# Third layer's attention: queries in the weighted heads' bank, probabilities scaled on GpSimd, keys first at the beginning

## The reference

```python
x = x + jnp.tanh(g_xattn[2]) * _L2_xattn_ref(_layernorm(x, axis=-1), ctx_2048, Wq, Wk, Wv, Wo)

def _L2_xattn_ref(inputs_q, inputs_kv, Wq, Wk, Wv, Wo):
    H, HD = (16, 128)
    q = (inputs_q @ Wq).reshape(b, sq, H, HD) * (1.0 / np.sqrt(HD))
    k = (inputs_kv @ Wk).reshape(b, skv, H, HD)
    v = (inputs_kv @ Wv).reshape(b, skv, H, HD)
    scores = jnp.einsum('bqhd,bkhd->bhqk', q, k)
    attn = jax.nn.softmax(scores, axis=-1)
    ctx = jnp.einsum('bhqk,bkhd->bqhd', attn, v).reshape(b, sq, H * HD)
    return ctx @ Wo
```

## Time and profile before

| | us |
|---|---|
| median of 3 runs (lowest, highest) | 3289.55 (3284.54, 3291.18) |
| profiled execution | 3289.13 |
| its span | 3287.4 |
| TensorE busy in the span | 2748.9 (84%) |
| VectorE busy | 2168.9 (66%) |
| ScalarE busy | 1652.4 (50%) |
| GpSimd busy | 872.1 (27%) |

### The profile page before, as it was taken

One profiled execution on the slowest core, in us unless ns is written; L12 is line 12 of the kernel. 1 busy time (PEld: TensorE's weight loads), 2 busy tenths in 40 slices (PEclk: granted clock), 3 DMA queues, 4 the chain that ended last, 5 costly groups with the idle time before them and its releaser, 6 DMA issues. The chain is left out here.

```text
span 3287.4 us, 47689 instructions
## 1 busy us (share of the span) xinstructions
PE 2748.9 (84%) x15136; PEld 1827.5 (56%) x15138; DVE 2168.9 (66%) x5020; ACT 1652.4 (50%) x3331; POOL 872.1 (27%) x1233
## 2 busy tenths in 40 slices
PE   7888995898899999835898989936689999957898
PEld 4334664777677777613787778714323323334676
DVE  5675336777676666566666666677988888577332
ACT  4453224677666777543444444412357777634222
POOL 0011003544522222002100010031189999402000
PEclk9798996999999999956999999967789999977899
DMA  2002003000000000011000000001000000020000
GB/s 58 1 2 88 1 0 116 26 1 14 14 1 8 7 1 1 1 34 58 23 10 20 7 13 1 1 20 39 7 1 2 1 1 2 1 98 2 1 0 13
DMA packets 37931, 57.24 MB, mean 17 GB/s; under 512 B 6400, under 2 KB 25792, under 8 KB 36416
## 3 DMA queue, kind: packets, MB, share of 16 engines
q1 hardware_dynamic: 37696, 54.35, 5.1%
HBM read 52.99 MB, written 1.05 MB: 16 GB/s over the span
## 5 line engine op out<-in xcount | busy, mean ns | idle before, releaser
L2891 ACT ACTIVATE a_exps<-psum,a_ln 128x512 f32<-128x512 f32 x512 | 334.4, 687 | 148.7 <-PE psum L2805 148.2
L2963 DVE TENSOR_REDUCE a_half_max<-psum 128x1 f32<-128x1024 f32 x256 | 304.4, 1215 | 46.4 <-PE psum L2789 45.1
L1975 DVE TENSOR_REDUCE a_neg_max<-psum 128x2 f32<-128x512 f32 (+1 forms) x128 | 122.5, 957 | 170.4 <-PE psum L1678 167.2
L1628 POOL TENSOR_TENSOR a_head_rstd<-a_head_var,neg_half 128x4 f32<-128x4 f32 x112 | 114.4, 1021 | 397.4 <-DVE a_head_var L1969 215.2
L1698 PE MATMUL psum<-a_probs_t,a_vals 128*128 128x256 f32 x768 | 191.9, 386 | 16.3 <-ACT a_probs_t L1855 16.3
L2723 POOL TENSOR_SCALAR a_stack<-a_xn_t 128x1024 bf16<-128x1024 f32 x175 | 193.6, 1106 | 27.1 <-POOL a_xn_t L2720 24.9
L847 DVE SCALAR_TENSOR_TENSOR f_silu<-f_silu,psum 128x352 f32<-128x352 f32 (+2 forms) x88 | 50.4, 572 | 227.0 <-ACT f_silu L820 226.8
L2805 PE MATMUL psum<-a_qs,a_ks 99*128 99x512 bf16 x512 | 190.4, 388 | 0.1
L1678 PE MATMUL psum<-a_k_t,a_q_t 128*128 128x256 f32 (+1 forms) x512 | 189.5, 493 | 0.9 <-ACT a_probs L1863 0.9
L1823 ACT ACTIVATE a_normed<-psum,a_head_bias,a_head_scale 128x128 f32<-128x128 f32 x448 | 168.9, 465 | 40.8 <-POOL a_head_bias L1633 39.7
L2720 POOL TENSOR_SCALAR a_xn_t<-a_exps 128x1024 f32<-128x1024 f32 x175 | 184.9, 1057 | 9.1 <-ACT a_exps L2891 9.1
(11 more groups left out here) (494 smaller groups left out, 6573.8 us busy)
## 6 DMA issues: line engine op xcount, KB each, us to landing
a_w_raw<-in_L_xattn_wproj_dram SPq DMA_DIRECT2D x8, 512.0 KB, 3.9
f_w_silu<-in_L_ffn_gate_dram SPq DMA_DIRECT2D x1, 2112.0 KB, 10.3
f_w_mul<-in_L_ffn_up_dram SPq DMA_DIRECT2D x1, 2112.0 KB, 14.9
a_probs<-in_ctx_t_dram SPq DMA_DIRECT2D x4, 512.0 KB, 5.1
f_w_silu<-in_L_ffn_Wu_dram SPq DMA_DIRECT2D x1, 2048.0 KB
f_w_mul<-in_L_ffn_Wg_dram SPq DMA_DIRECT2D x1, 2048.0 KB
f_w_down<-in_L_ffn_Wd_dram SPq DMA_DIRECT2D x1, 2048.0 KB, 17.6
a_q_raw<-in_L_xattn_wq_dram SPq DMA_DIRECT2D x4, 512.0 KB, 7.1
```

The source lines that it names most:

```text
L2891: act.activation(exps[:, n % UNITS, :], core.bank(LOGITS + n % LOGIT_BANKS), ACT.Exp, bias=ln255[:, :]).then_inc(exp_ready, 1)
L2963: v.tensor_reduce(half_max[:, h, t, half:half + 1], ring(("scores", s)), AX.X, ALU.max, negate=True).then_inc(ring_free, 1)
```

## The change

The order of the seven pieces becomes keys, values, queries, and then as before. The queries go to the bank of the weighted heads, `OUT_BANK`. V waits only for the values before (`v_ready`), Q for the heads' low part that last left the bank (`out_ready`) and for the queries before (`q_ready`); `weighted` gets a wait for the queries' low part of the step that it stands in. ScalarE and VectorE split in the new order. VectorE ends with the reciprocal and signals it (`recip_ready`); GpSimd scales the two tiles (`scale`), ahead of what it subtracts in that step. At the beginning GpSimd takes the root first and the context's low part after it; the weights' pieces are loaded and split in the order keys, values, queries, output; TensorE does the first keys between the two halves of the token transposes, and ScalarE copies the weights of the queries between the two halves of the tokens.

```diff
-        q_bank = lambda: core.bank(V_BANK)[:, 0:S]
-
-        WK, WQ, WV, WO = range(PIECES)
+        q_bank = lambda: core.bank(OUT_BANK)[:, 0:S]
+
+        WK, WV, WQ, WO = range(PIECES)
...
+                def scale(q):
+                    r = q % 2
+                    g.wait_ge(recip_ready, q + 1)
+                    for t in range(TB):
+                        last = g.tensor_scalar(probs[:, r, t, :], probs[:, r, t, :], recip[:, r, t:t + 1], 1.0, ALU.mult, ALU.mult)
+                    last.then_inc(probs_ready, 1)
+
+                rstd_gpsimd(core, g, shifted, rstd, var_ready, rstd_ready)
                 context_low(0)
-                rstd_gpsimd(core, g, shifted, rstd, var_ready, rstd_ready)
...
-                for q in range(STEPS):
-                    if context_at(q) is not None:
+                for q in range(STEPS + 1):
+                    if live(q, 1):
+                        scale(q - 1)
+                    if live(q, 0) and context_at(q) is not None:
                         context_low(context_at(q))
-                    if piece_at(q) is not None:
+                    if live(q, 0) and piece_at(q) is not None:
                         weight_low(piece_at(q))
...
-                    at_least(pe, v_ready, q)
+                    at_least(pe, out_ready, q - 3)
+                    at_least(pe, q_ready, q)
...
-                    pe.wait_ge(q_ready, q + 1)
+                    at_least(pe, v_ready, q)
...
                     pe.wait_ge(turn_ready, q + 1)
+                    pe.wait_ge(q_ready, min(q + 4, STEPS))
...
                     if live(q, 0):
+                        if q == 0:
+                            for t in range(NT // 2):
+                                turn_token(t)
+                        keys(q)
+                        if q == 0:
+                            for t in range(NT // 2, NT):
+                                turn_token(t)
+                        values(q)
+                        if q == 0:
+                            pe.wait_ge(token_ready, NT)
                         queries(q)
-                        keys(q)
-                        values(q)
...
                 weight_high(WK)
-                weight_high(WQ)
...
                 weight_high(WV)
+                for t in range(NT // 2):
+                    token(t)
+                weight_high(WQ)
+                for t in range(NT // 2, NT):
+                    token(t)
...
                     if live(q, 1):
                         v.wait_ge(exp_ready, q)
-                        v.reciprocal(recip[:, 1 - r, :], sums[:, 1 - r, :])
-                        v.drain()
-                        for t in range(TB):
-                            last = v.tensor_scalar(probs[:, 1 - r, t, :], probs[:, 1 - r, t, :], recip[:, 1 - r, t:t + 1], None, ALU.mult)
-                        last.then_inc(probs_ready, 1)
+                        v.reciprocal(recip[:, 1 - r, :], sums[:, 1 - r, :]).then_inc(recip_ready, 1)
```

More of the change, by code:

```diff
@@ L1103, in layer2_attention @@
         scores_full, max_ready, exp_ready, probs_ready = sem("scores_full"), sem("max_ready"), sem("exp_ready"), sem("probs_ready")
+        recip_ready = sem("recip_ready")
         turn_full, turn_high, turn_ready = sem("turn_full"), sem("turn_high"), sem("turn_ready")
@@ L1150, in load @@
                     else:
-                        src = feature_rows(dram["L2_xattn_" + ("Wk", "Wq", "Wv")[piece]])[:, :, n * QW:(n + 1) * QW]
+                        src = feature_rows(dram["L2_xattn_" + ("Wk", "Wv", "Wq")[piece]])[:, :, n * QW:(n + 1) * QW]
                         dst = w_raw[:, i % 2, :].rearrange("p (k n) -> p k n", k=DK)
@@ L1193, in _, with turn_token @@
             def _(pe):
-                for t in range(NT):
+                def turn_token(t):
                     at_least(pe, token_ready, t - 3)
@@ L1197, in _ @@
                     transpose_tile(core, pe, core.bank(t % 4), xn, t).then_inc(token_full, 1)
-                pe.wait_ge(token_ready, NT)
                 def keys(q):
@@ L1308, in _, with token @@
                 context_high(0)
-                weight_high(WK)
-                weight_high(WQ)
-                for t in range(NT):
+                def token(t):
                     act.wait_ge(token_full, t + 1)
                     act.copy(xn_parts[:, 0, :, t * P:(t + 1) * P], core.bank(t % 4)[:, 0:D].rearrange("p (k n) -> p k n", k=DK)).then_inc(token_high, 1)
+                weight_high(WK)
                 weight_high(WV)
+                for t in range(NT // 2):
[3 more added lines that the diff above has]
+                    token(t)
                 weight_high(WO)
@@ L1319, in _ @@
                     if live(q, 0):
-                        act.wait_ge(q_full, q + 1)
+                        act.wait_ge(k_full, q + 1)
                         at_least(act, scores_full, q - 1)
-                        act.mul(q_t[:, r, 0, :], q_bank(), SCALE).then_inc(q_high, 1)
-                        act.wait_ge(k_full, q + 1)
                         act.copy(k_t[:, r, 0, :], core.bank(K_BANK)).then_inc(k_high, 1)
@@ L1327, in _ @@
                         act.copy(vals[:, q // HPQ % 2, 0, q % HPQ, :], core.bank(V_BANK)).then_inc(v_high, 1)
+                        act.wait_ge(q_full, q + 1)
+                        act.mul(q_t[:, r, 0, :], q_bank(), SCALE).then_inc(q_high, 1)
                     if live(q, 2):
@@ L1358, in _ @@
                     if live(q, 0):
-                        v.wait_ge(q_high, q + 1)
-                        v.scalar_tensor_tensor(q_t[:, r, 1, :], q_bank(), SCALE, q_t[:, r, 0, :].bitcast(F32), ALU.mult, ALU.subtract).then_inc(q_ready, 1)
                         v.wait_ge(k_high, q + 1)
@@ L1365, in _ @@
                                         ALU.subtract).then_inc(v_ready, 1)
+                        v.wait_ge(q_high, q + 1)
+                        v.scalar_tensor_tensor(q_t[:, r, 1, :], q_bank(), SCALE, q_t[:, r, 0, :].bitcast(F32), ALU.mult, ALU.subtract).then_inc(q_ready, 1)
                     if q >= 2 * HPQ and q % HPQ == 0:
```

## The result

The changed kernel takes 3191.62 us (median of 4 runs, 3183.56 to 3200.37) against 3287.05 us of the kernel before (4 runs, 3284.24 to 3291.18): a ratio of 0.9705, with a 95% interval of 0.9689 to 0.9721. The forecast was 3195 us, the range 3183 to 3222. The profiled execution of the changed kernel is its fastest one, 3183.56 us with a span of 3181.8 us, so the two profiles stand 105.6 us apart and the medians 95.4. What belongs to the change must therefore be read from the stage itself, between its own marks.

The account below looks back on a forecast made before the run. An ordinary step was bound by a loop of 8.46 us through the queries' and values' shared bank, no engine busy throughout. Gains of 90.0 (middle) and 5 (beginning), minus 1 (end), take 3289.1 to 3195 us, range 3183 to 3222.

Parts of the forecast that it names:

- TensorE's own step: Step without waits: K keys, V values, Q queries, S scores, T transposes, W weighted values, P projection sum to 7.88 us.
- the middle stretch: Scores of step 0 to scores of step 63: 18.2 + 464.9 + 5.2, in all 488.3 us, gain 90.0.
- Part 1: Queries moved to the weighted heads' bank, order keys, values, queries: weighted values do not wait, 1.0 us to spare.
- Part 2: Scaling moved to GpSimd: a pair takes 1.35 us, costs nothing in the 59 full steps, nor up to 3.3 us.
- rival (b): Scaling on GpSimd held by VectorE, running only in its gaps, up to 6 us: 3355 us in all; chance 0.05.
- The long steps: Up to 15 of 62 steps, both scalings 3.05 instead of 0.88 us during GpSimd's subtraction; would become ordinary.
- Part 3: Beginning: new order and earlier root of the variances (1 to 2 us) gain 5 us, bounds 2 and 8.
- the second step gains more: Beginning, second step: its queries began 1.82 us after values' low part was asked for; together with the root 5 us.
- The end: Transposes of steps 62 and 63 wait for the scalings, about 0.5 us later twice: minus 1 us.
- (a): Wait only changes its place, before weighted values or elsewhere: steps stay 8.46 us, 3229 us in all; chance 0.12.
- (c): TensorE's clock at 0.96 in all 59 steps, not staying at 2.4 GHz: 19 us more, 3214 us; chance 0.08.
- (d): New order at the beginning brings nothing, queries still end when they did: 5 us less gain, 3200; no own chance.

Follow-up runs that it names:

- q_low_late: The changed kernel with VectorE making the queries' low part behind the maxima instead of ahead of them: 3257.72 us, ratio 0.9902.
- scale_only: The kernel before with only the scaling moved to GpSimd, old bank, order and beginning kept: 3210.74 us, ratio 0.9764.
- after: The changed kernel with the queries' new bank and order, scaling on GpSimd and new beginning: 3191.62 us, ratio 0.9705 to the kernel before.
- bank_only: The kernel before with only the queries' new bank and piece order, scaling still on VectorE, old beginning: 3199.36 us, ratio 0.9726.
- end_on_vector: The changed kernel with the scalings of the last two steps on VectorE as before: 3193.89 us in one execution.
- scale_four: The changed kernel with three more pairs of multiplications by 1.0 behind each pair of scalings on GpSimd: 3322.02 us, ratio 1.0097 to the kernel before.

## Why the prediction was right, point by point

**TensorE's own step.** Forecast 7.88, measured 7.85. From load to load in the step above: K 1.27, V 1.36, Q 0.82, S 1.28, T 0.99, W 1.42, P 0.71. S came out 0.11 shorter than in the earlier trace rows and Q, which now stands straight before it, 0.11 longer than there. The two misses cancel, so by luck the sum came out closer than its terms. That the pieces add up to a step, and that nothing else was behind the old waits, was the load-bearing step of the forecast, and it held to 0.4%. It made 1.9 us of the 2.5 by which the middle stretch is shorter than forecast (17.76 + 462.95 + 5.06 us where the forecast had 18.2 + 464.9 + 5.2).

**Part 1.** No wait of W, 1.0 us to spare: as forecast, and q_low_late shows that this 1.0 us is what the gain hangs on.

**Part 2.** A pair takes 1.36 us, forecast 1.35; it costs nothing in the full steps, and would not up to 3.3 us. VectorE's subtraction out of PSUM keeps its 0.69 us beside the pair (1806.13 above), and the pair its 1.36, so rival (b), a scaling held by VectorE, did not occur, nor did the pair hold VectorE. The Trainium skill (SBUF — State Buffer, Who interferes with whom) says that such VectorE instructions don't contend with GpSimd; here both sides agree with it, 0.69 us for the one and 691 to 701 ns for the other. The Trainium skill (GPSIMD Engine Reference, 3.1) gives 769 ns for 512 elements as a best case; the trace shows 694. The line drawn between the two groups of the earlier trace rows gave 677, 17 ns too little.

**The long steps.** Right in the result, incomplete in the reason. The hold of the earlier trace rows is one cause; scale_only shows a second, ScalarE's copy of the weight piece ahead of the queries' copy, which makes V late by 0.59 us even without the hold. In after the first is gone with the scaling, and the second is harmless, since W stands two pieces behind Q and V doesn't wait for it.

**Part 3.** The size was near, 6.2 against 5, inside the bounds; the split was wrong. The step that failed is "the second step gains more: its Q began 1.82 us after V's low part was asked for". That wait goes with the bank, and is worth 1.4 to 1.5 us. The larger part, 3.8 us by subtraction (6.2 less 1.4 for the bank and 1.0 for the root), is the first K taken while tokens are still being normalised and split, and V's weights being there before Q's. The prediction had mentioned this K and then counted it at nothing because the first Q would end about where it did. The first Q did start about there, 15.15 us after the statistics instead of 15.61; but in the new order the first K and V are done by then, where before they were still to come. The root's 1 to 2 us was 1.0.

**The end.** Forecast -1, measured -1.65. The two later scalings cost 0.98, as forecast; a clock that fell behind T's wait, which the prediction left out at this place, cost 0.66. That the clock falls there is not sure: in scale_only it did not, and the end cost 0.98.

**The rivals.** (a), a wait that only moves, and (c), a clock below full, did not come: no wait of W, and 1.00 over the whole middle stretch. (d) was half right about the first Q and wrong about the result. What the forecast did not ask is what each main part would bring alone: over four fifths of the 97 us, in either case.

## What to carry to other kernels

In a loop of engines, add up the bound engine's own pieces first: that sum is the floor, and an edit that takes the loop under it wins most of what there is (here 78.5 and 88.7 of 97 us), so that two edits of which each is enough don't add. Then count, for each new wait and each moved operation, how much later it could end before the bound engine notices; a slower engine is free as long as it stays inside that room, and an instruction placed too late by a microsecond is not. At the end of the loop the room is gone, and there the faster engine is worth keeping.

## What the runs showed of the hardware that I had not expected

- GpSimd's multiplication of a 128x512 tile takes 689 to 707 ns with a column of scalars and 614 to 634 ns with constants in its place.
- VectorE's eight normalisations out of SBUF take 6.71 us beside two GpSimd subtractions and 8.74 us with one more beside them, while its subtractions out of PSUM keep 0.69 us beside GpSimd's work of either kind. VectorE's pair of scalings in SBUF was held to 3.10 us again in bank_only; on GpSimd the same pair was never held.
- TensorE's clock at the wait before T of step 63: after a wait of 2.27 us (end_on_vector) it stayed at its upper level, 2.4 GHz (1.00 over the next 4.4 us). After one of 2.76 us it fell in after (a mean of 0.64, with W's weight loads taking 2.35 instead of 1.50 us) and stayed at 1.00 in scale_only. In scale_four TensorE waited 2.06 us in every step, and the clock was 1.00 from 1560 to 2000 us. The length of a wait alone did not tell whether the clock would fall.
